# Experts that gather their tokens and add their results onto the residual rows

## The reference, cut to what matters

```python
def _moe(x, w_router, wg, wu, wd):            # x: 4096 tokens, after an RMS norm
    probs = softmax(xf @ w_router)            # 8 experts
    topw, topi = top_k(probs, 2)              # two experts for each token
    topw = topw / sum(topw)
    g = silu(einsum("td,xdh->txh", xf, wg));  u = einsum("td,xdh->txh", xf, wu)
    eo = einsum("txh,xhd->txd", g * u, wd)    # hidden width 704
    out = einsum("txd,tx->td", eo, combine)   # combine holds the two weights of each token
y = h + _moe(_rmsnorm(h, g2), ...)            # and the kernel's output is the residual x1 + y
```

## Time and profile before

| | us |
|---|---|
| median of 3 runs | 3300.74 |
| the profiled execution's own time | 3297.82 |
| span of the profiled execution (first to last instruction) | 3296.2 |
| PE busy | 2698.5 (82%) |
| DVE busy | 1763.2 (53%) |
| ACT busy | 1458.2 (44%) |
| POOL busy | 490.7 (15%) |

### The profile page before, as it was taken

One profiled execution on the slowest core, in us unless ns is written; L12 is line 12 of the kernel. 1 busy time (PEld: TensorE's weight loads), 2 busy tenths in 40 slices (PEclk: granted clock), 3 DMA queues, 4 the chain that ended last, 5 costly groups with the idle time before them and its releaser, 6 DMA issues. The chain is left out here.

```text
span 3296.2 us, 55561 instructions
## 1 busy us (share of the span) xinstructions
PE 2698.5 (82%) x14654; PEld 1323.0 (40%) x14655; DVE 1763.2 (53%) x2832; ACT 1458.2 (44%) x2927; POOL 490.7 (15%) x650
## 2 busy tenths in 40 slices
PE   7996999999999999999949879887340299999980
PEld 5662232323232323233225434443340177777760
DVE  4565876767676767677436656664222022222223
ACT  2331576767676767677723336565010022222210
POOL 2444000000000000000014421110223300000006
PEclk9996899999999999999979979999665699999995
DMA  6777544444454444454035456653444211100116
GB/s 211 215 233 133 70 62 67 62 66 63 62 64 62 63 63 63 62 63 61 17 115 185 159 121 133 133 133 102 149 150 155 84 32 32 32 32 32 32 47 183
DMA packets 524784, 313.32 MB, mean 95 GB/s; under 512 B 312112, under 2 KB 486848, under 8 KB 524480
## 3 DMA queue, kind: packets, MB, share of 16 engines
q1 hardware_dynamic: 492752, 256.93, 38.6%
q0 software_dynamic: 11392, 37.76, 3.5%
q10 hardware_dynamic: 20464, 16.40, 1.6%
HBM read 188.91 MB, written 121.26 MB: 94 GB/s over the span
## 5 line engine op out<-in xcount | busy, mean ns | idle before, releaser
L719 DVE TENSOR_REDUCE att_cross_neg_max<-att_cross_ps_s 128x1 f32<-128x802 f32 x1024 | 965.6, 988 | 350.9 <-PE att_cross_ps_s L636 349.2
L794 ACT ACTIVATE att_cross_probs<-att_cross_ps_st 128x512 f32<-128x512 f32 (+1 forms) x1664 | 901.2, 599 | 394.7 <-PE att_cross_ps_st L655 382.2
L655 PE MATMUL att_cross_ps_st<-att_cross_q_pack,att_cross_k_pack 99*128 99x512 bf16 (+1 forms) x1664 | 575.0, 391 | 37.3 <-issue 28.4
L636 PE MATMUL att_cross_ps_s<-att_cross_k_pack,att_cross_q_pack 96*128 96x401 bf16 x2048 | 547.9, 350 | 70.1 <-DVE att_cross_neg_max L719 29.5
L670 PE MATMUL att_cross_ps_o<-att_cross_probs,att_cross_v_tiles 128*32 128x512 f32 (+1 forms) x3328 | 453.5, 618 | 1.0
L636 PEld LDWEIGHTS att_cross_ps_s<-att_cross_k_pack,att_cross_q_pack 96*128 96x128 bf16 x2048 | 176.8, 100 | 420.5 <-DVE att_cross_neg_max L719 204.9
L655 PEld LDWEIGHTS att_cross_ps_st<-att_cross_q_pack,att_cross_k_pack 99*128 99x128 bf16 (+1 forms) x1664 | 163.1, 100 | 415.5 <-ACT att_cross_probs L794 293.2
L719 DVE TENSOR_REDUCE att_self_neg_max<-att_self_ps_s 128x1 f32<-128x128 f32 (+3 forms) x512 | 236.2, 489 | 148.7 <-PE att_self_ps_s L639 145.7
L794 ACT ACTIVATE att_self_probs<-att_self_ps_st 128x256 f32<-128x256 f32 (+3 forms) x512 | 208.2, 441 | 142.4 <-PE att_self_ps_st L658 136.6
L1744 DVE COPY moe_hiddenT<-moe_ps_h 128x256 f32<-128x256 f32 x142 | 60.3, 425 | 296.9 <-PE moe_ps_h L1654 296.9
L636 PE MATMUL att_self_ps_s<-att_self_k_pack,att_self_q_pack 96*128 96x128 bf16 (+3 forms) x512 | 158.7, 312 | 56.4 <-DMA att_self_q_pack<-q_parts 25.1
(11 more groups left out here) (208 smaller groups left out, 2901.7 us busy)
## 6 DMA issues: line engine op xcount, KB each, us to landing
att_cross_k_pack<-k_parts SPq DMA_DIRECT2D x192, 200.1 KB, 7.5
k_parts<-in_part SPq DMA_DIRECT2D x72, 256.0 KB, 3.1
in_rows<-in_ctx_dram SPq DMA_DIRECT2D x24, 512.0 KB, 4.4
v_rows<-in_v_biased SPq DMA_DIRECT2D x24, 512.0 KB, 2.9
att_cross_q_pack<-q_parts SPq DMA_DIRECT2D x192, 64.0 KB, 7.7
att_cross_v_tiles<-v_rows SPq DMA_DIRECT2D x128, 96.0 KB
att_self_k_pack<-k_parts SPq DMA_DIRECT2D x192, 64.0 KB, 3.1
att_self_q_pack<-q_parts SPq DMA_DIRECT2D x192, 64.0 KB, 3.1
```

The lines of the kernel that those rows point to most:

```text
L636: last = nc.tensor.matmul(ps_s[bank][:, n, 0:w], qp[v.buf][0:SROWS, j, q * P:(q + 1) * P], kp[v.buf][0:SROWS, j, s:s + w], start=True, sto ...
L655: mm = nc.tensor.matmul(ps_st[bank_of_step[s]][0:rows, q0:SEQ], kp[u.buf][0:MROWS, j, t * P:t * P + rows], qp[u.buf][0:MROWS, j, q0:SEQ], ...
L719: nc.vector.tensor_reduce(nmax[v.odd][:, col, half:half + 1], ps_s[bank][:, 0:len(spans), 0:spans[0][1]], AX.XY, ALU.max, negate=True).the ...
L794: nc.scalar.activation(pr[0:rows, (u.odd * STEPS + s) % RING, q0:SEQ], ps_st[bank_of_step[s]][0:rows, q0:SEQ], ACT.Exp).then_inc(exp_done, 1)
```

## The change

`scatter_rows`, `combine` and `zeros_beside` go, with the DRAM tensors `in_sorted` and `out_sorted`. `route` also makes three tables by slot: token, target row and weight. `experts` gathers its rows from `hn_rows` by the token table, scales each result row by its weight, and adds it to its target row in DRAM (`sums`, the tensor that was `y_rows`, with 128 spare rows at its end for slots that no pair uses) by an indirect DMA that accumulates. At its end SP copies `sums` to `out`. Both indirect DMAs of a tile are POOL's; SP has no part in the loop. The loads of `wd` move from ACT in `scatter_rows` to SP in `route`.

The tables come from 64 float32 matmuls (32 tiles of tokens, two choices) summed in PSUM. For each, POOL makes a 128 x 128 matrix of 0 and 1 (lane of the slot) and DVE two 128 x 72 matrices (tile of the slot, times token number and times weight), in a ring of 4 buffers.

```diff
 def route(nc, wd, sums, keep, tokens):            # dve, after the slots are known
+                nc.vector.tensor_scalar(tile_i[:, :, :], slot_i[:, :, :], 7, None, ALU.arith_shift_right)
+                nc.vector.tensor_scalar(lane_i[:, :, :], slot_i[:, :, :], P - 1, None, ALU.bitwise_and)
...
+                for n in range(PAIRS_OF):          # 64
+                    if n >= RING:
+                        dve.wait_ge(slots_done, n - RING + 1)
+                    nc.vector.tensor_scalar(at_tile[n % RING][:, 0, :], keep["iota_tile"][:, 0:TILES],
+                                            tile_of[:, k, t:t + 1], keep["token"][:, t:t + 1], ALU.is_equal, ALU.mult)
+                    nc.vector.tensor_scalar(at_tile[n % RING][:, 1, :], keep["iota_tile"][:, 0:TILES],
+                                            tile_of[:, k, t:t + 1], weights[:, k, t:t + 1], ALU.is_equal, ALU.mult)\
+                      .then_inc(tile_ready, 1)
+                dve.wait_ge(slots_done, PAIRS_OF)
...
+            def _(pool):                           # 64 times
+                    nc.gpsimd.tensor_scalar(at_lane[n % RING][:, :], keep["iota_lane"][:, :], lane_of[:, k, t:t + 1], None,
+                                            ALU.is_equal).then_inc(lane_ready, 1)
...
+            def _(sp):                             # the 32 loads of wd, as ACT had them in scatter_rows
...
+            pe:                                    # 64 times
+                    nc.tensor.matmul(ps_slots[:, :, :].rearrange("p a t -> p (a t)"), at_lane[n % RING][:, :],
+                                     at_tile[n % RING][:, :, :].rearrange("p a t -> p (a t)"),
+                                     start=(n == 0), stop=(n == PAIRS_OF - 1)).then_inc(slots_done, 1)

-def experts(nc, in_sorted, out_sorted, keep, tiles):
+def experts(nc, hn_rows, sums, out, keep, tiles, tokens):
             def _(sp):
-                for t in range(3):
-                    load(Tile(0, t))
-                with sp.Fori(0, (tiles - 3) // 2) as i:
+                for i in range(2):
+                    sp.wait_ge(sent[i], 16 * ((tiles + 1 - i) // 2))
+                for c in range(4):
+                    rows = slice(c * tokens // 4, (c + 1) * tokens // 4)
+                    sp.dma_start(out[rows, :].rearrange("(p t) d -> p (t d)", p=P),
+                                 sums[rows, :].rearrange("(p t) d -> p (t d)", p=P)).then_inc(copied, 16)
+            def _(pool):
+                pool.sem_inc(turned, 2)
+                pool.sem_inc(added, 2)
+                def gather(t):
+                    pool.wait_ge(turned, t.n + 1)
+                    nc.gpsimd.tensor_copy(source[t.par][:, :], keep["slot_token"][:, bass.ds(t.n, 1)])\
+                      .then_inc(source_ready, 1)
+                    pool.wait_ge(source_ready, t.n + 1)
+                    pool.sem_inc(pool_turn, 1)
+                    pool.indirect_dma_start(out=rows[t.par][:, :], out_offset=None, in_=hn_rows,
+                                            in_offset=bass.IndirectOffsetOnAxis(ap=source[t.par][:, 0:1], axis=0))\
+                        .then_inc(rows_in[t.par], 16)
+                def add_up(t, first=False):
+                    if not first:
+                        pool.wait_ge(sent[1 - t.par], (t.i + (t.r + 1) // 2) * 16)
+                        pool.sem_inc(added, 1)
+                    nc.gpsimd.tensor_copy(target[t.par][:, :], keep["slot_target"][:, bass.ds(t.n, 1)])\
+                      .then_inc(target_ready, 1)
+                    pool.wait_ge(y_ready, t.n + 2)
+                    pool.wait_ge(target_ready, t.n + 1)
+                    pool.sem_inc(pool_turn, 1)
+                    pool.indirect_dma_start(out=sums, in_=y[t.par][:, :], in_offset=None, compute_op=ALU.add,
+                                            out_offset=bass.IndirectOffsetOnAxis(ap=target[t.par][:, 0:1], axis=0))\
+                        .then_inc(sent[t.par], 16)
+                for t in range(4):
+                    gather(Tile(0, t))
+                    if t >= 2:
+                        add_up(Tile(0, t - 2), t == 2)
+                with pool.Fori(0, (tiles - 5) // 2) as i:
+                    for r in range(2):
+                        gather(Tile(i, r + 4))
+                        add_up(Tile(i, r + 2))
+                gather(Tile(0, tiles - 1))
+                for t in range(tiles - 3, tiles):
+                    add_up(Tile(0, t))
             act, result(t):
-                    act.wait_ge(sent[t.par], (t.turn + 1) * 16)
-                    nc.scalar.copy(y[t.par][:, :], ps_y[:, :]).then_inc(y_ready, 1)
+                    act.wait_ge(added, t.n + 1)
+                    act.wait_ge(weight_ready, t.n + 1)
+                    nc.scalar.activation(y[t.par][:, :], ps_y[:, :], ACT.Copy, scale=weight[t.par][:, 0:1])\
+                       .then_inc(y_ready, 1)
             dve, before multiply(t, 0) of each step:
+                def take_weight(t):
+                    dve.wait_ge(y_ready, t.n)
+                    nc.vector.tensor_copy(weight[t.par][:, :], keep["slot_weight"][:, bass.ds(t.n, 1)])\
+                      .then_inc(weight_ready, 1)
```

More of the change, by code:

```diff
@@ L24 @@
 EXPERTS = 8
+SPARE_ROW = 8 * SEQ
 HIDDEN = 704
@@ L1320, in finish_self, with route @@
         p.clear()
-def route(nc, keep, tokens):
+def route(nc, wd, sums, keep, tokens):
     T = tokens // P
@@ L1553, in experts @@
         y = [p.sb(f"y{i}", [P, DIM]) for i in range(2)]
+        source = [p.sb(f"source{i}", [P, 1], I32) for i in range(2)]
+        target = [p.sb(f"target{i}", [P, 1], I32) for i in range(2)]
+        weight = [p.sb(f"weight{i}", [P, 1]) for i in range(2)]
         ps_g = [p.ps(f"ps_g{i}", [P, SEQ]) for i in range(2)]
@@ L1596, in _ @@
             def _(sp):
-                sp.sem_inc(turned, 2)
                 for i in range(2):
-                    sp.sem_inc(sent[i], 16)
-                def load(t):
-                    sp.wait_ge(turned, t.n + 1)
-                    sp.dma_start(rows[t.par][:, :], in_sorted[bass.ds(t.n * P, P), :]).then_inc(rows_in[t.par], 16)
-                def store(t):
-                    sp.wait_ge(y_ready, t.n + 2)
-                    sp.dma_start(out_sorted[bass.ds(t.n * P, P), :], y[t.par][:, :]).then_inc(sent[t.par], 16)
@@ L1612, in _ @@
                     for r in range(2):
-                        load(Tile(i, r + 3))
-                        store(Tile(i, r))
+                        gather(Tile(i, r + 4))
+                        add_up(Tile(i, r + 2))
+                gather(Tile(0, tiles - 1))
                 for t in range(tiles - 3, tiles):
-                    store(Tile(0, t))
-                for i in range(2):
-                    sp.wait_ge(sent[i], 16 * ((tiles + 1 - i) // 2 + 1))
+                    add_up(Tile(0, t))
@@ L1748, in first @@
                 def first(t):
+                    take_weight(t)
                     multiply(t, 0)
@@ L1965, in build @@
         project_inputs(nc, a["ctx"], a["x"], k_parts, v_rows, q_parts, keep, batches)
-        with ExitStack() as zeros_stack:
-            z, beside = zeros_beside(nc, in_sorted, zeros_stack, tiles, units)
-            attention(nc, q_parts, k_parts, v_rows, out_rows, CTX, False, keep, units, beside)
-            z.clear()
+        attention(nc, q_parts, k_parts, v_rows, out_rows, CTX, False, keep, units)
         invert_denominators(nc, out_rows, inverse, False, units)
```

258 lines of the change are left out of this document (80 added, 178 removed).

## The result

| | before | after |
|---|---|---|
| median of the runs | 3300.15 us (3298.1 to 3301.28, 4 runs) | 3786.51 us (3784.7 to 3788.45, 4 runs) |
| profiled execution: its time, span, clock | 3297.8, 3296.2, 0.909 | 3784.91, 3783.2, 0.880 |

The ratio is 1.1475, 95% interval [1.1455, 1.1495]: 14.75% slower. The forecast was 3693 us, 2.5% too low; its range, 3540 to 3860, holds the time. The increase was forecast at 392 us and is 486.

A forecast was written before the change was run, and what follows sets the result against it. PE alone was taken to bound `experts`. On the profiled 3297.8 us, + 537 (holes and clock) - 75.8 (`route`) - 67.4 (tail) - 1.3 (zero fills) gave 3690, as median 3693; range 3540 to 3860.

The forecast's parts named there:

- What bounds the kernel, and the order of the new loop: In `experts`, PE alone sets the pace; gather(t+2) queues behind add_up(t-1) on POOL, leaving a PE hole 68 times.
- The size of the hole: In `experts`, PE waits 5.7 us a tile for gathered rows; bounds 5.0 to 8.0.
- The clock: In `experts`, PE restarts at the lower clock after each hole, costing 2.2 us more a tile; bounds 0 to 2.2.
- Rival 1: In `experts`, the clock survives the hole: 3544 us in all; chance 0.12.
- Edits at nothing: In `experts`, ACT's scaled copy, DVE's `take_weight` and the new waits for `y_ready`, `added` and `sent` cost nothing.
- `route`: Table building, 64 rounds taking 25.6 us, then first gather 3.5; first transposes of `experts` 75.8 us earlier (37 to 82).
- Ahead of `route`: Before `route`, only the closing barrier of the 24 zero fills goes: 1.3 us less.
- Tail: After ACT's last result: last accumulate 3.6, copy 20, issue, landing and barrier 4; 67.4 us less (61 to 74).
- rival 2: In `experts`, the accumulate holds up the gather, making the hole 8.0 us: 3850 us in all; chance 0.19.
- rival 3: In `experts`, the gather isn't late, a tile stays at 8.21 us and only savings remain: 3156 us; chance 0.05.
- The turn of the sign: In `experts`, savings of 144.5 us equal 2.1 us for each of 68 tiles; any longer hole makes the kernel slower.
- The likeliest case: Whole kernel: the main forecast, hole and lower clock in each of 68 tiles, 3693 us, range 3610 to 3780; chance 0.64.

The follow-up runs named there:

- The first experiment: Changed kernel with gather(t+3) issued ahead of add_up(t) on POOL: 3179.06 us, ratio 0.9618 [0.959, 0.9646] to the kernel before.
- `e5_before_late_load`: Kernel before the change, with store(t) put ahead of load(t+3) on SP: 3613.37 us, beside 3295.96 for the kernel before.
- `e3_plain_write`: Changed kernel with a plain indirect write in place of the accumulating one, the sum left out: 3776.42 us.
- `e2b_pe_half_filled`: Changed kernel with 9 unneeded matmuls of 352 columns on PE at the end of each step: 3674.9 us.

## Why the prediction was right, and 94 us short

**What bounds the kernel, and the order of the new loop: right.** PE set the pace, the gather of tile t+2 stands behind `add_up(t-1)` on POOL, and PE's transposes wait for it in every tile from the fourth on. The first experiment removes the hole by that order alone, `e5_before_late_load` makes one by that order alone.

**The size of the hole: right in its chain, 1.2 us short.** The prediction counted from the moment when PE wanted the rows. Counted so, PE is 6.89 us late (6.73 of hole and 0.16 of overlap), and 5.66 were predicted. ACT's end is where it was put (0.34 us behind that moment, 0.32 predicted). Term by term, from ACT's end (means over the stage):

| step | predicted | measured |
|---|---|---|
| ACT's end to the accumulate's issue | 0.90 | 0.94 |
| accumulate, then the copy of the source column | 0.95 + 0.20 | 1.81 |
| copy's end to the gather's issue | 0.17 + 0.38 | 0.81 |
| gather's issue | 0.95 | 1.01 |
| from its end to PE's start | 1.79 | 1.98 |

The five steps sum to 6.55 us, 1.21 more than the 5.34. The mis-sized term is the second, by 0.66 us: the accumulate's issue is 1.60 us and not 0.95, and `e3_plain_write` shows that the addition is why; the copy ends 0.20 us behind it, as predicted. That this issue costs what a gather's costs was called a choice, as no row showed an accumulate. The third is 0.26 short: the row taken was POOL's wait from a small operation to a plain DMA, and to an indirect one it is 0.81 throughout. The landing's 1.98 is 0.19 more than the row's 1.79. The Trainium skill, DMA: Bandwidth & Descriptors, "Anatomy of one DMA — SWDGE (gpsimd) path", gives such a transfer about 2.0 us plus its bytes over 436 GB/s, for 128 KB an estimate of 2.3 us; this trace's 1.98 is below it.

**The clock: right, 0.2 us too dear.** 2.2 predicted, 2.0 measured. In the mean it falls 3.9 us after PE's last matmul (3.0 predicted) and is back 4.0 us after the restart (4.7 predicted); only the second number enters the cost. Rival 1, that the clock survives, is false: it fell in all 68 holes. In all the tile costs 604.9 / 68 = 8.9 us more, not 7.9: 68 of the 94 us.

**Edits at nothing: right.** No wait for `added` or the weight shows up in the tile; POOL's wait for `sent` does (0.37 us in the tile shown), but well ahead of the next result. ACT's scaled copy takes 0.47 us instead of 0.37, and ends 0.18 us behind PE's last matmul where the old one ended 0.16 behind it.

**`route`: 12.4 us short.** Up to the first round 21.8 us (22.3 predicted), the rounds 37.3 (25.6), behind them 1.85 (1.4), handover 1.55 (1.3), first gather 4.0 (3.5). The step that failed is POOL's operation "0.30 by the cast of 130": a comparison with a column of scalars takes it 0.58. The matmul's "below 0.34" was wrong too, as the four records of 1.35 us are two matmuls of 352 columns: a matmul of 144 columns takes 0.51 us from the start of its first record to the end of its second. That is still below POOL's 0.58, so it cost nothing. The range given, 19 to 64, holds the 37.3.

**Ahead of `route`: missed.** I had -1.3 for the zero fills and nothing else; it is +18.6. The widening of the tile of constants stood in the diff, and I did not price it. No row of before could have given the amount, but it belonged in the range.

**Tail: 5.7 us too long.** Accumulate to the copy's issue 4.9 us (3.6 predicted), copy and end 17.0 (24).

**Rivals 2 and 3: false.** The accumulate does not hold up the gather (1.90 us to PE's start with the addition, 1.92 without, 1.91 with the accumulate behind the gather). The gather was late, as forecast. The turn of the sign at 2.1 us a tile was not tested, and it was set too high: `route`, the stretch ahead of it and the tail make the savings 12.4 + 19.9 - 5.7 = 26.6 us smaller, 117.9 instead of 144.5, or 1.7 us for each of the 68 tiles. With no hole at all the kernel takes 3179 us, 23 more than rival 3's 3156.

**How much of the hit is the range.** The likeliest case's own range ended at 3780, and the 3786.5 measured lie just above it. The wide range holds them because its upper end was set with rival 2 in view, and rival 2 is false. The mechanism was right; most of its terms were short, and of the larger ones only the tail and the clock were too long.

## What to carry to other kernels

A queue that works in order turns its first late wait into everybody's wait. When transfers move to another engine's queue, write down for each fetch which wait stands ahead of it, and compare the moment that wait ends with the moment the bound engine wants the data; the fix can be a reordering of the same calls (here 3787 to 3179 us). The holes of 3.1 to 6.7 us that PE had here cost 1.5 to 2.8 us more than their length, nearly all of it because its clock fell in them or just behind them; those of 1.4 us hardly did.

## What the runs showed of the hardware that I had not expected

- An accumulating indirect DMA of 128 rows of 1 KB keeps POOL for 1.60 us, a plain one for 1.00; the small copy behind it ends 0.20 us later in both cases. The rows of the gather behind it land no later.
- A hole shortened by 0.6 us gave nothing: in `e3_plain_write` the period stayed at 17.1 us, because PE worked for 5.28 us at the lower clock instead of 3.98. In `e5_before_late_load` the clock fell only after PE had started again, behind 52 of 68 holes of 3.1 us, and stayed down for over 3 us of full work. Behind holes of 1.4 us (`e2b_pe_half_filled`) it fell in six of 68. The price of a hole is thus not proportional to its length.
- A float32 matmul of 352 columns is recorded twice (32 records for 16 matmuls): the "x4" of 1.35 us are two matmuls of 0.60.
- 644 B a partition of unused SBUF ahead of the constants cost 0.4% (ratio 1.0041 [1.0026, 1.0057]), with DMAs in the self-attention that take longer to land (3.1 us before, 3.5 padded). What about the place matters (alignment, the partitions' ends, the order of later tiles) stays open: one shift was tried, no second.
